# Dummy matmuls ahead of six stages, first groups taken through alone in two stages, and a routing norm one tile earlier

## The reference

```python
x = x + 0.5 * moe(LN(x))      # top-1 of 4 experts, 256 -> 1024, exact gelu, -> 256, + input, layer norm with gain
x = x + attention(LN(x))      # 16 heads of 16, causal softmax within each 1024 tokens
x = x + 0.5 * moe(LN(x))      # the same weights again
x = x + 0.5 * fp4_ffn(LN(x))  # down(silu(gate(x)) * up(x)), width 704
x = x + linear_attention(LN(x))
x = x + 0.5 * fp4_ffn(LN(x))
```

```python
def moe(x):                   # router logits, argmax, one expert per token
    e = argmax(x @ W_router)
    h = gelu(x @ W1[e] + b1[e])
    return layer_norm(h @ Wo + bo + x) * ln_gamma + ln_beta

def fp4_quant_dequant(x):     # per 16 values: scale = max|x| / 6, then the nearest of 0, .5, 1, 1.5, 2, 3, 4, 6
    ...

def fp4_linear(x, w):
    return fp4_quant_dequant(x) @ fp4_quant_dequant(w).T
```

## Time and profile before

| | us |
|---|---|
| median of three runs | 2276.48 (2274.24 to 2277.07) |
| the profiled execution | 2266.27 |
| its span (first to last instruction) | 2264.6 |
| TensorE busy | 2037.3 (90%) |
| VectorE busy | 1448.9 (64%) |
| ScalarE busy | 1021.6 (45%) |
| GpSimd busy | 921.9 (41%) |
| mean granted TensorE clock | 0.962 of full |

### The profile page before, as it was taken

How to read it: one execution, slowest core, us unless ns; L and a number is a source line. 1 busy time by engine, 2 the same in 40 slices (tenths; PEclk the granted TensorE clock), 3 DMA queues, 4 the chain that set the end, 5 groups by cost and what they waited for, 6 DMA issues and landing times. The chain is left out here.

```text
span 2264.6 us, 41707 instructions
## 1 busy us (share of the span) xinstructions
PE 2037.3 (90%) x13665; PEld 1410.6 (62%) x13665; DVE 1448.9 (64%) x3940; ACT 1021.6 (45%) x2367; POOL 921.9 (41%) x1143
## 2 busy tenths in 40 slices
PE   6699994989999999987899975999979999699998
PEld 6599992534444444356899973666656666467676
DVE  4342224768888888626674227998757666588885
ACT  4233331416666666744333322333326666433332
POOL 5222226621111111116122236666546666455553
PEclk9999996989999999997899997999999999899999
DMA  5465552554444444012555642000000000000000
GB/s 172 146 202 193 196 180 79 177 109 57 57 58 57 57 55 52 10 39 75 189 185 200 195 138 61 14 14 9 1 1 2 2 2 2 2 10 10 19 19 19
DMA packets 101709, 173.56 MB, mean 77 GB/s; under 512 B 14704, under 2 KB 66320, under 8 KB 101520
## 3 DMA queue, kind: packets, MB, share of 16 engines
q1 hardware_dynamic: 95376, 154.40, 26.2%
q0 software_dynamic: 6144, 16.79, 2.3%
HBM read 136.01 MB, written 34.87 MB: 75 GB/s over the span
## 5 line engine op out<-in xcount | busy, mean ns | idle before, releaser
L1106 DVE TENSOR_REDUCE a_part_max<-a_psS 128x1 f32<-128x512 f32 (+3 forms) x608 | 362.6, 655 | 79.3 <-PE a_psS L1036 70.7
L1162 ACT ACTIVATE a_PT<-a_psE 128x512 f32<-128x512 f32 (+1 forms) x608 | 309.3, 584 | 179.0 <-PE a_psE L1050 162.0
L577 PE MATMUL e_psH<-e_xsT,e_w 128*128 128x128 f32 x2240 | 265.8, 278 | 0.0
L577 PEld LDWEIGHTS e_psH<-e_xsT,e_w 128*128 128x128 f32 x2240 | 260.2, 195 | 0.1
L586 PE MATMUL e_psY<-wo_moe,e_gT 128*128 128x256 f32 x1120 | 253.0, 380 | 0.0
L1011 POOL TENSOR_SCALAR_AFFINE_SELECT a_PT<-a_PT 128x512 f32<-128x512 f32 x128 | 81.2, 634 | 409.2 <-ACT a_PT L1162 409.2
L1030 PE MATMUL a_psS<-sk,sq 96*128 96x512 bf16 (+3 forms) x768 | 232.7, 338 | 13.0 <-DMA sk<-qk_parts 8.2
L1050 PE MATMUL a_psE<-sq,sk 98*128 98x512 bf16 (+3 forms) x768 | 224.7, 330 | 4.1 <-DMA sq<-a_maxT 1.8
L586 PEld LDWEIGHTS e_psY<-wo_moe,e_gT 128*128 128x128 f32 x1120 | 207.9, 191 | 25.1
L608 ACT ACTIVATE e_gT<-e_psH,e_bias 128x128 f32<-128x128 f32 x560 | 159.6, 368 | 137.4 <-PE e_psH L577 134.4
L656 POOL TENSOR_TENSOR e_rstd<-e_moments,minus_half 128x1 f32<-128x1 f32 x70 | 45.2, 646 | 408.7 <-DVE e_moments L122 408.7
(11 more groups left out here) (295 smaller groups left out, 3781.4 us busy)
## 6 DMA issues: line engine op xcount, KB each, us to landing
e_w<-w_in SPq DMA_DIRECT2D x70, 1024.0 KB, 5.0
sq<-qk_parts SPq DMA_DIRECT2D x96, 128.0 KB, 6.0
sk<-qk_parts SPq DMA_DIRECT2D x96, 128.0 KB, 6.6
e_xs<-sorted_x SPq DMA_DIRECT2D x70, 128.0 KB, 2.0
e_xr<-sorted_x SPq DMA_DIRECT2D x70, 128.0 KB, 4.1
sorted_y<-e_yo SPq DMA_DIRECT2D x70, 128.0 KB, 1.7
X<-x_in SPq DMA_DIRECT2D x8, 512.0 KB, 6.4
qk_parts<-q_hi SPq DMA_DIRECT2D x32, 128.0 KB, 1.7
```

The costliest lines, as they stand in the source:

```text
L577: mm = pe.matmul(psH[p][:, n * P:(n + 1) * P], w1[p][:, k, n * P:(n + 1) * P], xsT[p][:, k, :], start=k == 0, stop=k == KD - 1)
L1106: dve.tensor_reduce(part_max[:, c, h0:h0 + heads, qt], psS[place % RING][:, 0:heads * n].rearrange("p (h k) -> p h k", h=heads), AX.X, ALU ...
L1162: act.activation(PT[kt % 2][:, h0:h0 + heads, q0:q0 + n], psE[e % RING][:, 0:heads * n].rearrange("p (h q) -> p h q", h=heads), ACT.Exp, s ...
```

## The change

- `keep_warm` issues matmuls of 128 x 512 in bf16 on constants into a PSUM bank whose content nobody reads, at the start of TensorE's queue in a stage: 14 in each expert stage, 45 in the projections, 70 in the first quantized FFN, 20 in the second, 8 in linear attention.
- Routing: ScalarE's `norm` runs at distance J + 3, which was J + 4; in each step it still stands behind `evacuate`.
- Projections: in GpSimd's queue relay of group g - 2 and the root of group 0 stand ahead of the gathers of group g; the other roots run at distance 3 (were 2), the parts at 6 (were 5).
- First quantized FFN: VectorE divides and rounds the first pair at distance 1, ahead of the measurement of the second pair; the other pairs stay at 3 and 4. GpSimd takes root and finishing step of the first pair at distances 2 and 4; the others' root is at 5 and their finishing step at 8 as before; `finish_h` stays at 12.

```diff
--- before.py
+++ after.py
@@ -105,6 +105,13 @@
 
 
 WEIGHT_LOADS = 9
+
+
+def keep_warm(pe, bank, st, passes):
+
+    for _ in range(passes):
+        pe.matmul(bank[:, 0:512], st.ident_bf[:], st.hide_k_after_q[:].unsqueeze(1).broadcast_to([P, 4, P]),
+                  start=True, stop=True)
 
 
 class Store:
@@ -398,7 +405,7 @@
                 act.activation(yT[p % 2][:].rearrange("p k q -> p (k q)"), psY[:, 0:D], ACT.Copy).then_inc(yevac, 1)
 
             pipeline(act, TILES, ([(0, evacuate_y)] if after_attention else []) +
-                     [(J + 5, evacuate), (J + 4, norm)], unroll=4, loop=False)
+                     [(J + 5, evacuate), (J + 3, norm)], unroll=4, loop=False)
 
         @block.gpsimd
         def _(pool):
@@ -555,6 +562,7 @@
 
         @block.tensor
         def _(pe):
+            keep_warm(pe, psY[0], st, 14)
 
             def turn(t, p):
                 pe.wait_ge(x_in[p], 8 * (t - p) + 16)
@@ -779,6 +787,14 @@
                 pool.tensor_tensor(rstd[p][:], moments[p][:, :, 1], st.minus_half[:].broadcast_to([P, G]),
                                    ALU.pow).then_inc(rooted, 1)
 
+            def root_first(g, p):
+                if g == 0:
+                    root(g, p)
+
+            def root_later(g, p):
+                if g > 0:
+                    root(g, p)
+
             def parts(g, p):
                 for c in range(CH):
                     pool.wait_ge(rest, 2 * (g * CH + c + 1))
@@ -787,8 +803,8 @@
                     pool.tensor_tensor(low[c][:], remainder[c % 2][:], mid[c][:],
                                        ALU.subtract).then_inc(cut, 1)
 
-            pipeline(pool, NG, [(0, lambda g, p: gather.start(pool, g)), (1, lambda g, p: gather.relay(pool, g)),
-                                (2, root), (5, parts)], loop=False)
+            pipeline(pool, NG, [(2, lambda g, p: gather.relay(pool, g)), (2, root_first),
+                                (0, lambda g, p: gather.start(pool, g)), (3, root_later), (6, parts)], loop=False)
 
         @block.sync
         def _(sp):
@@ -816,6 +832,8 @@
 
         @block.tensor
         def _(pe):
+            keep_warm(pe, psQ[0], st, 45)
+
             def turn(g, p):
                 for j in range(G):
                     pe.wait_ge(normed, g * G + j + 1)
@@ -1425,9 +1443,20 @@
                 dve.scalar_tensor_tensor(out=st.X[:, t, :], in0=psY[:, 0:D], scalar=0.5, in1=st.X[:, t, :],
                                          op0=ALU.mult, op1=ALU.add).then_inc(added, 1)
 
-            pipeline(dve, TILES, [(8, multiply), (8, divide_h), (10, add), (0, measure, 2), (3, divide_x, 2), (4, round_x, 2),
-                                  (8, round_h)],
-                     unroll=4)
+            def first(t):
+
+                return gathers and isinstance(t, int) and t == 0
+
+            def later(stage):
+                return lambda t, p: None if first(t) else stage(t, p)
+
+            def quantize_first(t, p):
+                if first(t):
+                    divide_x(t, p)
+                    round_x(t, p)
+
+            pipeline(dve, TILES, [(8, multiply), (8, divide_h), (10, add), (1, quantize_first), (0, measure, 2),
+                                  (3, later(divide_x), 2), (4, later(round_x), 2), (8, round_h)], unroll=4)
 
         @block.gpsimd
         def _(pool):
@@ -1466,9 +1495,15 @@
             stages = [(1, root, 2), (8, finish_h), (4, finish_x, 2)]
             if gathers:
 
-                stages = [(k + 4, *rest) for k, *rest in stages]
-                stages = [(0, lambda t, p: gather.start(pool, t // 2), 2),
-                          (2, lambda t, p: gather.relay(pool, t // 2), 2)] + stages
+                def at_first(stage):
+                    return lambda t, p: stage(t, p) if t == 0 else None
+
+                def later(stage):
+                    return lambda t, p: None if t == 0 else stage(t, p)
+
+                stages = [(0, lambda t, p: gather.start(pool, t // 2), 2), (2, lambda t, p: gather.relay(pool, t // 2), 2),
+                          (2, at_first(root), 2), (4, at_first(finish_x), 2),
+                          (5, later(root), 2), (12, finish_h), (8, later(finish_x), 2)]
             pipeline(pool, TILES, stages, unroll=4, loop=not gathers)
 
         @block.scalar
@@ -1508,6 +1543,7 @@
 
         @block.tensor
         def _(pe):
+            keep_warm(pe, psGate, st, 70 if gathers else 20)
             pe.wait_ge(padded, 2)
 
             def turn(t, p):
@@ -1797,6 +1833,8 @@
 
         @block.tensor
         def _(pe):
+            keep_warm(pe, psQ, st, 8)
+
             def pair(t, p):
 
                 pe.wait_ge(kevac, KEVAC * (t + 1))
```

## The result

The changed kernel takes 2270.91 us (median of 14 runs, 2267.65 to 2275.95) against 2274.94 us (14 runs, 2273.27 to 2277.07): a ratio of 0.9982 with an interval of 0.9975 to 0.9989. That is 4.0 us less. The forecast was 3.0 us less than 2276.48, so 2273.5. It forecast no difference beyond 0.2%, and by the median there is none, though the interval reaches 0.25%. The gain itself is clear of the noise.

The account below looks back on a forecast made before the run. TensorE, busy 2037.3 of 2264.6 us, was taken to leave little inside nine barrier-separated stages. Terms -4.5 + 0 - 1.8 - 2.4 + 5.0 + 2.0 - 1.3 + 0 = -3.0 gave 2273.5 us, range 2269.0 to 2280.5.

Parts of the forecast that it names:

- first routing: First routing stage: earlier norms save 2.0 us, then 0.52 in each of 5 groups; -4.5 us, bounds 1 and 5.5.
- first experts: First expert stage: passes raise TensorE's clock, so tile 0's up-projection takes 3.74 instead of 5.52 us; -1.8 us.
- second experts: Second expert stage: passes raise TensorE's clock, so tile 0's up-projection takes 3.74 instead of 6.11 us; -2.4 us.
- projections: Projection stage: root 1 stands behind four more gathers, the first projection starts later, nothing absorbs it; +5.0 us, bounds 4 and 6.
- first quantized FFN: First quantized FFN: root 2 comes 4.9 us later, delaying tile 0's evacuation and the first product; +2.0 us.
- linear attention: Linear attention: eight passes hold the clock, first q/k projection takes 1.9 instead of 3.23 us; -1.3 us.
- rival 3: First quantized FFN: the late root is absorbed in idle time and pair 0's head start counts; -6.0, 2270.5 us; chance 0.12.
- the smaller wait for the ranks: First routing: VectorE's wait for rank counts falls from 1.33 to 0.81 us, so a group takes 6.33 instead of 6.85.
- rival 2: Routing gains only its first 2 us, scatters and counts staying in the 6.85 us rhythm; -0.5, 2276.0 us; chance 0.16.
- Rival 1: Passes do not hold the clock, the gap ahead of each burst lowers it; +2.5, 2279.0 us; chance 0.18.
- Rival 4: Projection stage: delayed in GpSimd's queue, but TensorE catches up 3 us or more; -6, 2270.5 us; chance 0.04.
- rival 5: Projections and first quantized FFN: first groups miss the change's aim, losing full bounds 6 and 4.9; +0.9, 2277.4 us; chance 0.10.

Follow-up runs that it names:

- experiment 5: The kernel before with only GpSimd's new order in the projection stage: 2279.76 us, ratio 1.0018.
- experiment 6: The changed kernel with GpSimd's old order in the projection stage, its 45 passes kept: 2264.22 us, ratio 0.9955.
- experiment 12: Changed kernel with GpSimd's old projection order and, in the first quantized FFN, the second pair's root directly behind the first pair's finishing step: 2263.23 us, ratio 0.9952.
- experiment 1: The kernel before, unchanged, run and profiled once more: 2275.5 us, ratio 0.9998.
- experiment 9: The kernel before with only the routing norm at J + 3, 14 passes per expert stage and 8 in linear attention: 2264.59 us, ratio 0.9955.
- experiment 2: The changed kernel with the routing norm back at J + 4 in the second routing stage alone: 2270.12 us, ratio 0.9975.

## Why the prediction was right

The parts, forecast against the means of the profiles with and without each part. Left out are the first profile of before in the two routing rows, and in the projections the two profiles in which ScalarE's first copy came late:

| part | forecast, us | measured, us |
|---|---|---|
| first routing | -4.5 | -5.3 |
| second routing | 0 | -0.7 |
| first experts | -1.8 | -1.7 |
| second experts | -2.4 | -1.5 |
| projections | +5.0 | +5.8 |
| first quantized FFN | +2.0 | +1.3 |
| linear attention | -1.3 | -1.1 |
| second quantized FFN | 0 | 0 |
| sum (before rounding) | -3.0 | -3.1 |

With the left-out profiles in, the three rows are -4.8, +0.3 and +4.9, and the sum is -2.6. Both sums and the medians' 4.0 us lie within the interval (2.5 to 5.7).

The sum is better than its terms. Seven of them are off by up to 0.9 us, some one way and some the other, and that the errors cancel to a few tenths is luck. As a time, 2270.91 lies just outside the 2271 to 2275.5 given for the forecast by itself and close to rival 3's 2270.5. This does not speak for the rival: the median of before came out 1.5 us lower in 14 runs than in the three that the forecast started from, and the stage that rival 3 is about became longer, not shorter.

- **Routing.** The step that the smaller wait for the ranks, 0.81 us, would be what stays gave 6.33 us a group; 6.31 was measured, and the waits of 0.81 are there. The mechanism was right, and rival 2, in which the groups stay 6.85 us apart, is out. The size is off by 0.8 us. The last root came 5.0 us earlier, not 4.5: the first of the five groups gained 0.85 us where 0.52 was forecast, the others 0.52 to 0.59. The roots stand at the same places in all five profiles with the old order (the last at 50.98 to 51.03), so this does not come from the choice of profile. The rest, 0.3 us, lies behind the last root, and its cause is open. What the choice of profile did hide is the stop: the prediction read the 16 scatters as "without a gap", while there is one of 0.76 us in that profile and one of 2.5 to 2.8 us in all others, with either order.
- **Expert stages.** The passes hold the clock where the gap behind them is short (1.59 and 1.75 us in the changed kernel, 3.74 us for both first up-projections; the same 3.74 in all 13 stages whose gap was 0.9 to 2.2 us). Rival 1, that the gap brings it down, is true in single executions: at 2.71 us of idle time it fell, behind 4.35 us too, and at 3.69 us it did not. One of these bursts took 5.36 us, above the 5 us that the prediction named as a sign of being wrong. The mean gain is therefore 3.1 and not 4.2 us. What decides the gap is when the second tile's rows land.
- **Projections.** Right in mechanism and size. Root 1 behind four more gathers was forecast "some 26 us after its first gather", and is 26.7. Alone it makes the kernel 4.3 us slower (experiment 5), and without it the change gives 11 instead of 4 us (experiment 6). This is the one part that should be undone. The price came 0.4 higher at the projection (5.4) and the rest of it in the stage's tail. Rival 4, that TensorE catches up, is out.
- **First quantized FFN.** Second root 4.3 us later where 4.9 was forecast, evacuation of tile 0 1.9 us later where 2.9 was forecast, and about 1.3 us at the end where 2.0 was. Over all profiles with and without the pair (without experiment 12) root and evacuation are 4.8 and 2.4 us later, and the first product 1.7, so the chain of waits is as described. Two sums in it are slightly off: 1373.2 + 2.3 + 2.5 is 1378.0 and not 1378.2, and 2.9 - 0.8 is 2.1 and not 2.0. Rival 3, in which the head start of pair 0 counts, does not hold. Of rival 5 only the half on the projections came near (5.8 of its 6 us); at the FFN's end stand 1.3 and not 4.9 us.
- **Linear attention.** The first projection gave its 1.25 us in five of nine profiles, and less or nothing in four. Where it did, the stage took 295.1 to 295.6 us, otherwise 296.4 to 297.3; without the passes it took 295.5 to 298.8. What decides is not known.

What I had wrong beside the sizes is the scale on which I read the profile: I took one execution's routing stages as the kernel's own. The median of the runs was there, 10.2 us above the profiled time, and I noted the distance without asking where it lay. Here it did little harm: the roots of the first stage, from which the forecast was made, stand at the same times in both profiles of before.

What stays open is why ScalarE's first copy in the projection stage came late in two of the four profiles that had passes there and the old order (22.2 us with 45 passes, 25.1 us with 70), and never in the ten profiles without them or with the late root. The passes are the common element, and a larger number went with a longer stop; with 45 it was there once in three. That it is the arrival of ScalarE's instructions would be a guess from the missing releaser alone, and no run shows it: the few transfers on the instruction queues do not tell the late cases from the others.

## What to carry to other kernels

Profile the unchanged kernel twice before you price a stage: where the profiled time and the median differ by more than the effect sought, one stage of that profile is not typical. A matmul without a reader paid in all 13 expert stages where real work followed within 2.2 us and TensorE then ran on without a break; it is uncertain before a wait whose end varies, and a large number of them may go with a late start of another engine. When a helper engine's queue is reordered to bring one item forward, count how many slow items (here gathers of 1.26 us) now stand ahead of the next item of the same kind, for that one sets the stage.

## What the runs showed of the hardware

- ScalarE and VectorE stood still until 63.7 and 63.8 us for 2.5 and 2.0 us with all that they read done (experiment 1), VectorE in the changed kernel for 3.8 us. A wait of VectorE without a releaser stands at this place of the first routing stage in 13 of 14 profiles. The one without it is also the one whose second routing stage is short, and its two stages together are 7.7 us shorter than in the second profile of the same kernel. The cause is not known.
- The granted clock fell in a stretch without matmuls of 2.71 us (experiment 9: 0.55 on average in the microsecond from 1084, 0.50 in that from 1086) and held over one of 3.69 us (experiment 2, second expert stage: 3.74 us for the up-projection behind it). Behind one of 4.35 us it fell 0.7 us after the up-projection had begun (experiment 2). The Trainium skill ("TensorE: Matmul & The Clock Gate", "Why this matters for your kernels") warns of idle gaps of a few microseconds. The traces agree that this is the scale, and show that near it the same expert stage gains in one execution and loses in the next.
- 24 passes took 7.5 and 8.2 us and 14 took 4.8 to 6.1 us: the first ones run at the lower of the two levels, and how many do differs between executions. The granted clock rose 4.9 us behind the first pass in the changed kernel's first expert stage, at 79.76, when 12 had begun, and 3.5 us behind it in experiment 12's, when 9 had.
